# The first layer's two attentions in units of two chunks: a new order of work on five engines

## The chip, the cores and the metric
The kernel runs on one core of a Trainium2 chip. A core has TensorE (PE, matrix products into the banks of PSUM), VectorE (DVE), ScalarE (ACT), GpSimd (POOL) and SyncE (SP, which only issues DMA transfers). Each engine takes its own instructions in order and they wait for each other by semaphores. The metric is the device time of one execution in microseconds, the lower the better.

## The reference
Two transformer layers on x (4 batches, 512 tokens, 256 features) with a context of 1601 rows of 192 features. The change touches the first layer's two attentions:
```python
# layer 0: 16 heads of 64; B = 4, N = 512; S = 512 (self) or 1601 (cross, xc = context)
x = _attn(_ln(x, g1, b1), _ln(x, g1, b1), Wq1, Wk1, Wv1, Wo1, bo1) + x
x = _attn(_ln(x, g2, b2), context, Wq2, Wk2, Wv2, Wo2, bo2) + x
...
    scores = jnp.einsum('bnhd,bshd->bhns', q, k) * scale
    attn = jax.nn.softmax(scores, axis=-1)
    out = jnp.einsum('bhns,bshd->bnhd', attn, v)
```
The second layer has the same with 16 heads of 16. Everything is in float32; the kernel splits q, k and the output into a high and a low part (`q_hi`, `q_lo`, ...) and sums products of the parts.

## The kernel before
The program is a row of phases: projections (`project_phase`), then an attention, five and four in turn. `attend_phase` does self0 (phase a0, 4 chunks of 128 keys) and cross0 (a1, 13 chunks, the last with 65 keys); `attend_narrow` does the second layer's self1 (a2) and cross1 (a3). In a0 and a1 the work is cut into NG = 32 groups of two heads of one batch. For a group:

- Maxima ("items"): for each head, each of the four 128-row pieces of q, and each block of keys (one of 512, or four of 402), TensorE makes scores with all 128 rows, k_hi and k_lo stacked against q_hi twice, into `mx`; VectorE reduces them (L1198).
- `row`: four transposes (L1017) turn a head's maxima into a row of `aux`, and ScalarE copies it, negated, into row 64 of `q_second` (L1131).
- `scores`: per chunk and head two products into a bank of `sc`, the stacked one (L1029) and one of 65 rows, k_hi by q_lo with the maxima subtracted (L1030). ScalarE makes the exp of a bank into `prob` (L1148).
- `values`: per chunk two products, one per head, into the two column halves of `pv` (L1041; each is recorded as two matmuls).
- Sums: GpSimd adds the probabilities of chunk pairs (L977, and L984 in self0), VectorE the last chunk's and the two halves (L1212, L1223 in cross0). Two products with ones (L1056) give the denominators, ScalarE copies them (L1161), VectorE takes reciprocals in four pieces (L1230), multiplies (`divide`, L1246), ScalarE casts the high part (L1168), VectorE subtracts for the low part (L1254), SP stores both.

Each group has U = 2 NCP steps (a chunk pair of one head). In a step TensorE alternates a score with an item of the next group, and the late steps of earlier groups are placed in chosen steps: `value_at`, `DEN_AT`, `RECIP_AT`, `DIVIDE_AT`, `HIGH_AT`, `LOW_AT`. SP loads a group's q, k and v SLOTS - 1 groups ahead (SLOTS 4 or 3), when the values of an earlier one are done. `attend_narrow` already makes maxima for two heads at once in row halves (L1479) and sends them through DRAM (L1380, L1387).

## Time and profile before
| | us |
|---|---|
| median of 3 runs | 3969.08 |
| lowest and highest | 3967.0, 3972.28 |
| the profiled execution | 3972.02 |
| its span, first to last instruction | 3970.2 |
| busy: PE, DVE, ACT, POOL | 3472.6, 2430.1, 2003.7, 1125.2 |
| self0, from the first load to the end (195 to 613): PE busy | 396.48 of 418 |
| cross0 (1025 to 2195): PE busy | 1143.68 of 1170 |

Positions in the trace are microseconds from the span's start. PE is the time in which a matmul was under way; matmuls overlap, so from one's start to the next one's start is what it costs. PEclk is the granted clock of TensorE as a share of 2.4 GHz.

### The profile page before, as it was taken

To read this page: it belongs to the slowest core of one execution; us is meant where nothing else is said; L and a number is where in the kernel's file an instruction comes from. 1 tells how busy PE (TensorE), PEld (TensorE's weight loads), DVE (VectorE), ACT (ScalarE), POOL (GpSimd) and SP (SyncE) were. 2 spreads that over 40 slices of the span, in tenths; PEclk is the share of its full clock that TensorE was granted. 3 is DMA by queue.
4 is the path that set the end of the run, shared out by engine and by line. 5 is a ranking of instruction groups with operands and counts; after the bars stand their busy time and mean duration, and the time that the engine had idled before them with its cause. 6 is when DMAs were issued, how large, how long until landed. Compare 5 with 4: busy or idle time off the path is not lost. (4 is left out here: it accounts for less than half of the span.)

```text
span 3970.2 us, 57943 instructions
## 1 busy us (share of the span) xinstructions
PE 3472.6 (87%) x17596; PEld 2019.0 (51%) x17596; DVE 2430.1 (61%) x4148; ACT 2003.7 (50%) x3541; POOL 1125.2 (28%) x539
## 2 busy tenths in 40 slices
PE   7899995999799999999999588588488599999776
PEld 5644443888455555555554456333366444444254
DVE  4368884443477777777776344386254399999333
ACT  4356662445355555555555223167344168888633
POOL 0056660000366667766667000012000000000000
PEclk8999997999799999999999799789799789999888
DMA  6787766999855555555552432234454522222121
GB/s 213 270 187 194 194 161 247 332 318 312 217 134 134 124 125 132 134 139 122 123 130 57 151 111 96 80 113 133 147 193 139 148 77 87 95 95 100 58 85 42
DMA packets 363425, 590.63 MB, mean 149 GB/s; under 512 B 43675, under 2 KB 196859, under 8 KB 362151
## 3 DMA queue, kind: packets, MB, share of 16 engines
q1 hardware_dynamic: 362312, 586.05, 51.0%
q10 hardware_dynamic: 958, 2.62, 0.4%
q8 instruction: 85, 1.39, 0.1%
q14 instruction: 70, 0.57, 0.0%
HBM read 345.71 MB, written 239.97 MB: 148 GB/s over the span
## 5 line engine op out<-in xcount | busy, mean ns | idle before, releaser
L1198 DVE TENSOR_REDUCE a_blk_max<-a_mx 128x1 f32<-128x402 f32 (+1 forms) x1280 | 734.0, 587 | 430.5 <-PE a_mx L1001 411.5
L1148 ACT ACTIVATE a_prob<-a_sc 128x512 f32<-128x512 f32 (+1 forms) x1088 | 640.1, 597 | 505.1 <-PE a_sc L1030 470.2
L1569 ACT ACTIVATE a_prob<-a_sc 128x512 f32<-128x512 f32 (+1 forms) x1088 | 585.9, 598 | 136.6 <-PE a_sc L1492 131.0
L977 POOL TENSOR_TENSOR a_prob_sum<-a_prob,a_prob_sum 128x1024 f32<-128x1024 f32 x256 | 617.7, 2414 | 62.8 <-ACT a_prob L1148 53.7
L1041 PE MATMUL a_pv<-a_prob,a_v 128*64 128x512 f32 (+1 forms) x2176 | 585.9, 617 | 0.0
L1596 DVE TENSOR_REDUCE a_blk_max<-a_mx 128x1 f32<-128x402 f32 x1024 | 512.1, 568 | 73.6 <-PE a_mx L1479 69.4
L1001 PE MATMUL a_mx<-a_k_stack,a_q_stack 128*128 128x402 f32 (+1 forms) x1280 | 485.0, 389 | 38.2 <-DMA a_q_stack<-q_hi_cross 23.5
L1029 PE MATMUL a_sc<-a_q_stack,a_k_stack 128*128 128x512 f32 (+1 forms) x1088 | 460.5, 423 | 2.1 <-ACT a_q_second L1131 2.1
L1030 PE MATMUL a_sc<-a_q_second,a_k_second 65*128 65x512 f32 (+1 forms) x1088 | 432.1, 397 | 0.0
L977 POOL TENSOR_TENSOR a_prob_sum<-a_prob 128x1024 f32<-128x1024 f32 x128 | 312.1, 2448 | 417.8 <-ACT a_prob L1148 417.8
L1001 PEld LDWEIGHTS a_mx<-a_k_stack,a_q_stack 128*128 128x128 f32 x1280 | 247.8, 194 | 291.7 <-DVE a_blk_max L1198 109.6
L1479 PE MATMUL a_mx<-a_k_stack,a_q_stack 63*128 63x402 f32 (+1 forms) x1280 | 300.5, 409 | 79.9 <-DMA a_q_stack<-a_prob 61.9
L1510 PE MATMUL a_pv<-a_prob,a_v 128*32 128x256 f32 (+2 forms) x4096 | 347.4, 412 | 8.9 <-ACT a_o_full L1548 7.5
L742 DVE TENSOR_TENSOR p_split_lo<-p_ps,p_split_hi 128x512 fp32r<-128x512 f32 (+2 forms) x280 | 171.5, 622 | 296.2 <-ACT p_split_hi L630 295.3
L1029 PEld LDWEIGHTS a_sc<-a_q_stack,a_k_stack 128*128 128x128 f32 (+1 forms) x1088 | 203.2, 187 | 263.5 <-ACT a_prob L1148 132.5
L1492 PE MATMUL a_sc<-a_q_stack,a_k_stack 64*128 64x512 f32 (+1 forms) x1088 | 301.6, 500 | 8.6 <-ACT a_prob L1569 8.5
L630 ACT CAST p_split_hi<-p_ps 128x512 fp32r<-128x512 f32 (+2 forms) x280 | 147.5, 534 | 271.0 <-PE p_ps L355 116.0
L1492 PEld LDWEIGHTS a_sc<-a_q_stack,a_k_stack 64*128 64x128 f32 (+1 forms) x1088 | 118.8, 184 | 254.9 <-ACT a_prob L1569 202.5
L1479 PEld LDWEIGHTS a_mx<-a_k_stack,a_q_stack 63*128 63x128 f32 x1280 | 181.9, 199 | 127.5 <-issue 63.3
L1230 DVE RECIPROCAL a_den<-a_den 128x128 f32<-128x128 f32 x256 | 235.6, 933 | 11.5 <-ACT a_den L1161 11.5
L1455 POOL TENSOR_TENSOR a_o_full<-a_o_full,a_inv 128x512 f32<-128x512 f32 x32 | 40.8, 1276 | 611.6 <-DMA a_inv<-inverse 611.6
L1030 PEld LDWEIGHTS a_sc<-a_q_second,a_k_second 65*128 65x128 f32 (+1 forms) x1088 | 203.0, 187 | 10.6
(248 smaller groups left out, 4911.3 us busy)
## 6 DMA issues: line engine op xcount, KB each, us to landing
a_v<-v_cross SPq DMA_DIRECT2D x48, 768.0 KB
a_k_stack<-k_hi_cross SPq DMA_DIRECT2D x32, 801.0 KB, 6.7
a_k_stack<-k_lo_cross SPq DMA_DIRECT2D x32, 801.0 KB, 9.8
a_k_second<-k_hi_cross SPq DMA_DIRECT2D x32, 801.0 KB
v_cross<-p_v_sb SPq DMA_DIRECT2D x48, 512.0 KB, 4.1
k_hi_cross<-p_split_hi SPq DMA_DIRECT2D x120, 200.0 KB, 3.3
k_lo_cross<-p_split_lo SPq DMA_DIRECT2D x120, 200.0 KB, 3.2
a_q_stack<-q_hi_self SPq DMA_DIRECT2D x64, 256.0 KB, 4.9
```

Source lines behind the costliest of these rows:

```text
L977: nc.gpsimd.tensor_tensor(prob_sum[:, h], prob_of(c, cp, h), other, ALU.add)\
L1001: nc.tensor.matmul(mx[:, (c * NI + m) % MXB, 0:a.blk], qst[r][0:rows, h, t * P:(t + 1) * P], kst[r][0:rows, h, at:at + a.blk], start=True, ...
L1029: nc.tensor.matmul(out, kst[r][:, h, k0:k0 + rows], qst[r][:, h, :], start=True, stop=False)
L1030: nc.tensor.matmul(out, k2[r][0:ROWS, h, k0:k0 + rows], q2[r][0:ROWS, h, :], start=not wide, stop=True).then_inc(st_done, 1)
L1041: last = nc.tensor.matmul(pv[h * M:(h + 1) * M, :], v[r][0:rows, j, h * M:(h + 1) * M], prob_of(c, cp, h)[0:rows, j % 2, :], start=(j == 0 ...
L1148: nc.scalar.activation(prob_of(c, cp, h)[0:rows, k, :], sc[0:rows, (c * E + e) % SCB, :], ACT.Exp, scale=a.scale).then_inc(exp_done, 1)
L1198: nc.vector.reduce_max(blk_max[:, r, h, t, nb:nb + 1], mx[:, (c * NI + n) % MXB, 0:a.blk], AX.X)\
L1479: nc.tensor.matmul(mx[:, g % MXB, 0:a.blk], qst[i % SLOTS][rows, j, t * P:(t + 1) * P], kst[i % SLOTS][rows, j, at:at + a.blk], start=True ...
L1492: nc.tensor.matmul(sc[0:keys, e % SCB, :], kst[i % SLOTS][rows, j, ch * P:ch * P + keys], qst[i % SLOTS][rows, j, :], start=True, stop=Tru ...
L1510: last = nc.tensor.matmul(pv[32 * h:32 * h + 32, cols], v[i % SLOTS][0:keys, ch, 32 * h:32 * h + 32], prob[0:keys, tau % RC, h, cols], sta ...
L1569: nc.scalar.activation(prob[0:keys, tau % RC, m, :], sc[0:keys, e % SCB, :], ACT.Exp, scale=a.scale).then_inc(exp_done, 1)
L1596: nc.vector.reduce_max(dst, mx[:, g % MXB, 0:a.blk], AX.X).then_inc(item_read, 1)
```

## The change
`attend_phase` goes, and `attend_wide` does self0 and cross0. The work is now in units w of two chunks of a group, T = 32 x NCP of them (NCP is 2 in self0 and 7 in cross0).

- TensorE, per unit: four scores (chunk by chunk, head by head), the first part of the unit's maxima, the values of unit w - 1, the denominators if they are due, the rest of the maxima. `pairs_by(w)` says how many pairs of maxima are made by the end of unit w: a group's are complete LEAD = 3 units before it starts. `cut(w)` halves a unit's.
- Maxima: one pair is one piece of q by one block of keys for both heads, the one in rows 0 to 63 and the other in rows 64 to 127, from the high parts alone. The second head's k is stacked the other way round for this.
- VectorE collects the maxima in `row_max`, transposes it in 32 x 32 blocks (`turn`), SP stores it in DRAM and loads it as row 64 of `q_second`; k's row 64 is -1.
- Denominators: two products with ones, into a bank of `mx`. VectorE transposes the bank, takes 16 reciprocals per partition and transposes them back with a broadcast (`invert`). The copy by ScalarE and the long reciprocals go.
- Banks: `mx` 4 and `sc` 3 in both (before 4 and 2 in self0, 3 and 3 in cross0); `aux` goes. SLOTS is 5 in self0 (4 before), 3 in cross0. `sc` is freed by its exp, `prob` (4 or 3 units) by `prob_free`.
- k comes in four transfers of 64 rows instead of two. SP's order per group is in the loop below.
- In `attend_narrow` the scratch for maxima and inverses has another layout, so that rows are read back whole.

The diff, cut to its core:
```diff
-        self.maxima = [dram(f"maxima{n}", [P, 32], F32) for n in range(2)]
-        self.inverse = [dram(f"inverse{n}", [4, NQ], F32) for n in range(2)]
+        self.maxima = [dram(f"maxima{n}", [32, P], F32) for n in range(2)]
+        self.inverse = [dram(f"inverse{n}", [32, P], F32) for n in range(2)]
...
-def attend_phase(pr, name, a):
...
-                sp.dma_start(pr.maxima[n % 2], row_turned[:, n % 2, :]).then_inc(max_stored[n % 2], 16)
+                sp.dma_start(pr.maxima[n % 2].rearrange("c (b i) -> b c i", b=4), row_turned[:, n % 2, :])\
+                    .then_inc(max_stored[n % 2], 16)
...
-                dst = qst[n % SLOTS][63:P:64].rearrange("p j (t b i) -> p (j t) b i", t=4, b=4)
-                src = pr.maxima[n % 2].rearrange("(b x c) i -> x c b i", x=4, c=8)
-                sp.dma_start(words(dst), src[0:2]).then_inc(row_loaded[n % 2], 16)
+                sp.dma_start(words(qst[n % SLOTS][63:P:64]),
+                             pr.maxima[n % 2][0:16].rearrange("(r j t) i -> r j (t i)", r=2, j=2))\
+                    .then_inc(row_loaded[n % 2], 16)
...
-                sp.dma_start(pr.inverse[n % 2].rearrange("h (x i) -> (h x) i", x=32), den[:, n % OS, :])\
+                sp.dma_start(pr.inverse[n % 2][0:16].rearrange("c (y i) -> (c y) i", i=16), den[:, n % OS, :])\
                     .then_inc(inv_stored, 16)
...
-                sp.dma_start(inv[:, n % OS, :], pr.inverse[n % 2].rearrange("(h u) n -> h u n", u=1)
-                             .to_broadcast([4, 32, NQ])).then_inc(inv_loaded[n % OS], 16)
+                rows = pr.inverse[n % 2][0:16].rearrange("(h u c) i -> h u (c i)", h=4, u=1)
+                sp.dma_start(inv[:, n % OS, :], rows.to_broadcast([4, 32, NQ])).then_inc(inv_loaded[n % OS], 16)
...
+def attend_wide(pr, name, a):
...
+    SLOTS = 3 if a.cross else 5
+    RC = 3 if a.cross else 4
+    OS = 3 if a.cross else 4
+    PAIRS = 4 * NB
+    NI = 2 * PAIRS
...
+    MXB, SCB = 4, 3
+    LEAD = 3
+    T = NG * NCP
+    LAST = a.chunk_rows(NC - 1)
+    NV = 1 + (LAST < P)
+    DEN_AT, DIVIDE_AT, HIGH_AT = NCP + 2, NCP + 3, NCP + 4
+    pool_sums = [(cp, h) for cp in range(1, min(NCP, 6)) for h in range(2)]
+    dve_sums = [(cp, h) for cp in range(6, NCP) for h in range(2)]
...
+    def pairs_by(w):
+        return min(NG * PAIRS, -(-PAIRS * (NCP + LEAD + w + 1) // NCP))
+    def cut(w):
+        return (pairs_by(w - 1) + pairs_by(w) + 1) // 2
+    def place(p):
+        return p + sum(cut(i * NCP + DEN_AT) <= p for i in range(NG))
+    def den_place(i):
+        return cut(i * NCP + DEN_AT) + i
...
+        kst = [sb(f"k_stack{s}", [P, 2, KP], F32R) for s in range(SLOTS)]
+        qst = [sb(f"q_stack{s}", [P, 2, NQ], F32R) for s in range(SLOTS)]
+        k2 = [sb(f"k_second{s}", [65, 2, KP], F32R) for s in range(SLOTS)]
+        q2 = [sb(f"q_second{s}", [65, 2, NQ], F32R) for s in range(SLOTS)]
+        v = [sb(f"v{s}", [P, NC, P]) for s in range(SLOTS)]
+        prob = sb("prob", [P, RC, 2, 2, BANK])
+        prob_sum = sb("prob_sum", [P, 2, 2, BANK])
+        CS = 1 if a.cross else 2
...
+        mx = st.enter_context(nc.psum_tensor(f"{name}_mx", [P, MXB, BANK], F32))
+        sc = st.enter_context(nc.psum_tensor(f"{name}_sc", [P, SCB, BANK], F32))
+        pv = st.enter_context(nc.psum_tensor(f"{name}_pv", [P, BANK], F32))
...
+            def load_kq(n):
+                s = n % SLOTS
+                if n >= SLOTS:
+                    sp.wait_ge(st_done, (n - SLOTS + 1) * E)
+                (k_hi, k_lo), q_hi = (t[n] for t in pr.k[a.name]), pr.q[a.name][0][n]
+                for h in range(2):
+                    for half, part in enumerate((k_hi, k_lo) if h == 0 else (k_lo, k_hi)):
+                        sp.dma_start(words(kst[s][64 * half:64 * half + 64, h]), part[64 * h:64 * h + 64])\
+                            .then_inc(loaded[s], 16)
+                for half in range(2):
+                    sp.dma_start(words(qst[s][64 * half:64 * half + 64]), q_hi.rearrange("(h r) s -> r h s", h=2))\
+                        .then_inc(loaded[s], 16)
+            def load_second(n):
+                s, k_hi, q_lo = n % SLOTS, pr.k[a.name][0][n], pr.q[a.name][1][n]
+                for dst, src in ((k2[s], k_hi), (q2[s], q_lo)):
+                    sp.dma_start(words(dst[0:64]), src.rearrange("(h r) s -> r h s", h=2)).then_inc(loaded2[s], 16)
...
+            def store_maxima(n):
+                sp.wait_ge(turned, n + 1)
+                if n >= 2:
+                    sp.wait_ge(row_loaded[n % 2], 16 * (n // 2))
+                sp.dma_start(pr.maxima[n % 2].rearrange("c (b i) -> b c i", b=4), row_turned[:, n % 2, :])\
+                    .then_inc(max_stored[n % 2], 16)
+            def load_maxima(n):
+                sp.wait_ge(max_stored[n % 2], 16 * (n // 2 + 1))
+                sp.dma_start(words(q2[n % SLOTS][64:65]), pr.maxima[n % 2][0:8].rearrange("(o h t) i -> o h (t i)", o=1, h=2))\
+                    .then_inc(row_loaded[n % 2], 16)
...
+            for n in range(SLOTS - 1):
+                load_kq(n)
+                load_second(n)
+                load_v(n)
+                if n == 0:
+                    store_maxima(0)
+                    load_maxima(0)
+            for i in range(NG + 3):
+                if a.cross:
+                    at(load_kq, i + SLOTS - 1)
+                    at(load_second, i + SLOTS - 1)
+                    at(load_v, i + SLOTS - 1)
+                    at(store_maxima, i + 1)
+                    at(load_maxima, i + 1)
+                    at(store, i - 1)
+                else:
+                    at(store_maxima, i + 1)
+                    at(load_maxima, i + 1)
+                    at(load_kq, i + SLOTS - 1)
+                    at(load_second, i + SLOTS - 1)
+                    at(load_v, i + SLOTS - 1)
+                    at(store, i - 3)
...
+            def add(i, m):
+                cp, h = pool_sums[m]
+                pool.wait_ge(exp_done, step_of(i, cp, 1, h) + 1)
+                if cp == 1:
+                    if i:
+                        pool.wait_ge(merged, (i - 1) * 2 + h + 1)
+                    other = prob_of(i * NCP, h)
+                else:
+                    pool.wait_ge(pool_sum, i * len(pool_sums) + m - 1)
+                    other = prob_sum[:, h]
+                nc.gpsimd.tensor_tensor(prob_sum[:, h], prob_of(i * NCP + cp, h), other, ALU.add)\
+                    .then_inc(pool_sum, 1)
+            def merge(i, h):
+                pool.wait_ge(pool_sum, i * 2 + h + 1)
+                if i >= CS:
+                    pool.wait_ge(den_done, i - CS + 1)
+                nc.gpsimd.tensor_tensor(chunk_sum[:, i % CS, h, :], prob_sum[:, h, 0, :], prob_sum[:, h, 1, :], ALU.add)\
+                    .then_inc(merged, 1)
+            for i in range(NG):
+                for m in range(len(pool_sums)):
+                    add(i, m)
+                    if not dve_sums:
+                        merge(i, m)
...
+            def maxima(p0, p1):
+                for p in range(p0, p1):
+                    i, t, nb = pair_of(p)
+                    if p % PAIRS == 0:
+                        pe.wait_ge(loaded[i % SLOTS], 16 * 6 * (i // SLOTS + 1))
+                    for h in range(2):
+                        n = 2 * place(p) + h
+                        if n >= MXB:
+                            pe.wait_ge(item_read, n - MXB + 1)
+                        rows, at = slice(64 * h, 64 * h + 64), a.block_at[nb]
+                        nc.tensor.matmul(mx[:, n % MXB, 0:a.blk], qst[i % SLOTS][rows, h, t * P:(t + 1) * P],
+                                         kst[i % SLOTS][rows, h, at:at + a.blk], start=True, stop=True)\
+                            .then_inc(item_done, 1)
...
+            def scores(w, k, h):
+                i, cp = divmod(w, NCP)
+                s, ch, e = i % SLOTS, 2 * cp + k, step_of(i, cp, k, h)
+                if cp == 0 and k == 0 and h == 0:
+                    pe.wait_ge(loaded2[s], 32 * (i // SLOTS + 1))
+                    pe.wait_ge(row_loaded[i % 2], 16 * (i // 2 + 1))
...
+                if e >= SCB:
+                    pe.wait_ge(exp_done, e - SCB + 1)
+                out = sc[0:keys, e % SCB, :]
+                nc.tensor.matmul(out, kst[s][:, h, k0:k0 + keys], qst[s][:, h, :], start=True, stop=False)
+                nc.tensor.matmul(out, k2[s][:, h, k0:k0 + keys], q2[s][:, h, :], start=False, stop=True)\
+                    .then_inc(st_done, 1)
...
+            def denominators(i):
+                n = 2 * den_place(i)
+                pe.wait_ge(merged, 2 * (i + 1))
+                pe.wait_ge(item_read, n - MXB + 1)
+                for h in range(2):
+                    last = nc.tensor.matmul(mx[64 * h:64 * h + 64, n % MXB, :], pr.ones[:, 0:64],
+                                            chunk_sum[:, i % CS, h, :], start=True, stop=True)
+                last.then_inc(den_done, 1)
...
+            maxima(0, pairs_by(-1))
+            for w in range(T):
+                for ch in a.pair(w % NCP):
+                    for h in range(2):
+                        scores(w, ch % 2, h)
+                maxima(pairs_by(w - 1), cut(w))
+                if w:
+                    values(w - 1)
+                sums_at(w)
+                maxima(cut(w), pairs_by(w))
...
+            def high_part(i):
+                act.wait_ge(divided, i + 1)
...
+            def prob_free(w, h):
+                i, cp = divmod(w, NCP)
+                act.wait_ge(pv_done, i * NC + min(NC, 2 * cp + 2))
+                one = (max(cp, 1), h)
+                if one in pool_sums:
+                    act.wait_ge(pool_sum, i * len(pool_sums) + pool_sums.index(one) + 1)
+                else:
+                    act.wait_ge(dve_sum, i * len(dve_sums) + dve_sums.index(one) + 1)
+            for w in range(T):
+                i, cp = divmod(w, NCP)
+                if cp == 1 and i:
+                    raw_copy(i - 1)
+                if w >= HIGH_AT and (w - HIGH_AT) % NCP == 0:
+                    high_part((w - HIGH_AT) // NCP)
+                for ch in a.pair(cp):
+                    keys = a.chunk_rows(ch)
+                    for h in range(2):
+                        if w >= RC and ch % 2 == 0:
+                            prob_free(w - RC, h)
+                        e = step_of(i, cp, ch % 2, h)
+                        act.wait_ge(st_done, e + 1)
+                        nc.scalar.activation(prob_of(w, h)[0:keys, ch % 2, :], sc[0:keys, e % SCB, :],
+                                             ACT.Exp, scale=a.scale).then_inc(exp_done, 1)
...
+            def turn(i):
+                dve.wait_ge(item_read, 2 * place(i * PAIRS + PAIRS - 1) + 2)
+                if NB > 1:
+                    nc.vector.reduce_max(row_max[:, i % 2, 0:8], blk_max[:, i % 2], AX.X).then_inc(max_done, 1)
...
+                nc.vector.transpose(row_turned[:, i % 2, :], row_max[:, i % 2, :]).then_inc(turned, 1)
...
+            def invert(i):
+                n = 2 * den_place(i)
+                dve.wait_ge(den_done, i + 1)
+                nc.vector.transpose(den[:], mx[:, n % MXB, :]).then_inc(item_read, 2)
+                dve.wait_ge(item_read, n + 2)
+                nc.vector.reciprocal(inv_cols[:], den[:].rearrange("p (k i) -> p k i", i=32)[:, :, 0])\
+                    .then_inc(inverted, 1)
+                dve.wait_ge(inverted, i + 1)
+                nc.vector.transpose(inv[:], inv_cols[:].rearrange("p (k o) -> p k o", o=1).to_broadcast([P, 16, 32]))\
+                    .then_inc(inv_turned, 1)
...
+            def last_sums(i):
+                for n, (cp, h) in enumerate(dve_sums):
+                    rows = a.chunk_rows(2 * cp)
+                    dve.wait_ge(exp_done, step_of(i, cp, 0, h) + 1)
+                    dve.wait_ge(pool_sum, (i + 1) * len(pool_sums) - 2 + h + 1)
+                    nc.vector.tensor_tensor(prob_sum[0:rows, h, 0, :], prob_sum[0:rows, h, 0, :],
+                                            prob_of(i * NCP + cp, h)[0:rows, 0, :], ALU.add).then_inc(dve_sum, 1)
+                if i >= CS:
+                    dve.wait_ge(den_done, i - CS + 1)
+                for h in range(2):
+                    dve.wait_ge(dve_sum, 2 * i + h + 1)
+                    nc.vector.tensor_tensor(chunk_sum[:, i % CS, h, :], prob_sum[:, h, 0, :], prob_sum[:, h, 1, :],
+                                            ALU.add).then_inc(merged, 1)
...
+            def divide(i):
+                dve.wait_ge(pv_copied, i + 1)
+                dve.wait_ge(inv_turned, i + 1)
...
+            blocks(0, pairs_by(-1))
+            for w in range(T + HIGH_AT):
+                blocks(pairs_by(w - 1), cut(w))
+                late(invert, w, DEN_AT)
+                blocks(cut(w), pairs_by(w))
+                if dve_sums:
+                    late(last_sums, w, NCP + 1)
+                late(divide, w, DIVIDE_AT)
+                late(low_part, w, HIGH_AT)
...
         project_phase(pr, "p0", x_in=ins["x"],
                       attn=(SELF0, w0 + "g1", w0 + "b1", w0 + "Wq1", w0 + "Wk1", w0 + "Wv1"))
-        attend_phase(pr, "a0", SELF0)
+        attend_wide(pr, "a0", SELF0)
         project_phase(pr, "p1", x_in=ins["x"], x_out=pr.x, after=(SELF0, w0 + "Wo1", w0 + "bo1"),
                       attn=(CROSS0, w0 + "g2", w0 + "b2", w0 + "Wq2", w0 + "Wk2", w0 + "Wv2"))
-        attend_phase(pr, "a1", CROSS0)
+        attend_wide(pr, "a1", CROSS0)
         project_phase(pr, "p2", x_in=pr.x, x_out=pr.x, after=(CROSS0, w0 + "Wo2", w0 + "bo2"),
                       ff=("geglu", w0 + "g3", w0 + "b3", w0 + "Wp", w0 + "bp", w0 + "Wf", w0 + "bf"),
                       attn=(SELF1, w1 + "n1_g", w1 + "n1_b", w1 + "sq_w", w1 + "sk_w", w1 + "sv_w"))
```

## Rows read from the trace of the kernel before
**Rows 1.** Windows of self0 and cross0 in steady state: busy us (instructions), granted clock, DMA share, GB/s.
```profile
300.00:550.00 250.00, 250.00 (x1071) 122.29 (x1067) 206.59 (x289) 152.65 (x268) 161.56 (x82) 1.00 0.78 193
1200.00:2000.00 800.00, 800.00 (x3350) 409.65 (x3348) 570.97 (x997) 419.08 (x703) 545.03 (x228) 1.00 0.56 131
```
**Rows 2.** Timeline of TensorE in self0: start, us, line, operands, count.
```profile
402.40 1.08 PE L1041 MATMUL a_pv<-a_prob,a_v 128*64 128x512 f32 x4
403.31 1.03 PE L1056 MATMUL a_aux<-a_chunk_sum,ones 128*64 128x512 f32 x4
404.27 0.50 PE L1029 MATMUL a_sc<-a_q_stack,a_k_stack 128*128 128x512 f32 x1
...
404.84 0.39 PE L1001 MATMUL a_mx<-a_k_stack,a_q_stack 128*128 128x512 f32 x1
405.07 0.39 PE L1029 MATMUL a_sc<-a_q_stack,a_k_stack 128*128 128x512 f32 x1
...
405.77 0.60 PE L1017 MATMUL a_aux<-ident,a_blk_max 128*1 128x128 f32 x4
406.30 1.08 PE L1041 MATMUL a_pv<-a_prob,a_v 128*64 128x512 f32 x4
407.31 0.50 PE L1001 MATMUL a_mx<-a_k_stack,a_q_stack 128*128 128x512 f32 x1
...
415.49 1.03 PE L1056 MATMUL a_aux<-a_chunk_sum,ones 128*64 128x512 f32 x4
```
**Rows 3.** Timeline of TensorE in cross0.
```profile
1488.16 1.03 PE L1056 MATMUL a_aux<-a_chunk_sum,ones 128*64 128x512 f32 x4
...
1514.52 0.34 PE L1001 MATMUL a_mx<-a_k_stack,a_q_stack 128*128 128x402 f32 x1
1514.70 0.40 PE L1029 MATMUL a_sc<-a_q_stack,a_k_stack 128*128 128x512 f32 x1
...
1523.48 1.03 PE L1056 MATMUL a_aux<-a_chunk_sum,ones 128*64 128x512 f32 x4
```
**Rows 4.** Groups by line in cross0, 1200 to 2000: busy us, mean ns, idle before.
```profile
L1198 DVE TENSOR_REDUCE a_blk_max<-a_mx 128x1 f32<-128x402 f32 x725 | 404.9, 567 | 227.6 <-PE a_mx L1001 214.0
...
L1212 DVE TENSOR_TENSOR a_prob_sum<-a_prob_sum,a_prob 65x512 f32<-65x512 f32 x44 | 28.1, 679 | 0.0
L1246 DVE TENSOR_TENSOR a_o_full<-a_o_full,a_den 128x512 f32<-128x512 f32 x23 | 22.3, 971 | 0.0
```
**Rows 5.** Groups by line in self0, 300 to 550.
```profile
L1148 ACT ACTIVATE a_prob<-a_sc 128x512 f32<-128x512 f32 x166 | 94.4, 595 | 24.8 <-PE a_sc L1030 17.9
...
L1246 DVE TENSOR_TENSOR a_o_full<-a_o_full,a_den 128x512 f32<-128x512 f32 x20 | 27.4, 1369 | 0.0
```
**Rows 6.** Timeline at the start of self0 and of cross0.
```profile
194.60 0.74 SPq L926 DMA_DIRECT2D a_k_stack<-k_hi_self  x1
...
201.93 3.99 PE L1001 MATMUL a_mx<-a_k_stack,a_q_stack 128*128 128x512 f32 x8 [12.75 <-DMA a_q_stack<-q_hi_self]
...
207.13 0.47 PE L1029 MATMUL a_sc<-a_q_stack,a_k_stack 128*128 128x512 f32 x1 [0.77 <-ACT a_q_second L1131]
...
1037.76 15.81 PE L1001 MATMUL a_mx<-a_k_stack,a_q_stack 128*128 128x402 f32 x32 [23.46 <-DMA a_q_stack<-q_hi_cross]
...
1055.19 0.76 PE L1029 MATMUL a_sc<-a_q_stack,a_k_stack 128*128 128x512 f32 x1 [0.77 <-ACT a_q_second L1131]
```
**Rows 7.** Timeline of TensorE in cross1, two pairs and the product after them.
```profile
3401.68 0.70 PE L1479 MATMUL a_mx<-a_k_stack,a_q_stack 63*128 63x402 f32 x4
3402.31 0.64 PE L1510 MATMUL a_pv<-a_prob,a_v 128*32 128x256 f32 x8
```
**Rows 8.** Timeline of TensorE in self1, after an idle piece.
```profile
2659.24 0.50 PE L1479 MATMUL a_mx<-a_k_stack,a_q_stack 63*128 63x512 f32 x2 [1.79 <-DMA a_q_stack<-q_lo_self]
```
**Rows 9.** Window of self1 just after it: busy us, granted clock, DMA share, GB/s.
```profile
2659.80:2663.20 3.40, 3.40 (x22) 1.13 (x20) 2.57 (x5) 1.59 (x3) 0.06 (x1) 0.50 0.03 11
```
**Rows 10.** DMA issues in cross1, 3200 to 3700: count, KB, median us to landing.
```profile
maxima<-a_row_turned SPq DMA_DIRECT2D x14, 16.0 KB, 1.4
```

556 lines of the change are left out of this document (122 added, 434 removed).

## The prediction
> **What bounds the kernel now.** I read the windows first, at the two attentions of the first layer, which the change rewrites. [rows 1] In steady state TensorE is busy 250.00 of 250.00 us in the self attention and 800.00 of 800.00 us in the cross attention, at a granted clock of 1.00. VectorE is busy 83% and 71%, ScalarE 61% and 52%, GpSimd 65% and 68%. TensorE is the bound, and only what is on TensorE, or stops it, sets the time. The period of a group (two heads of one batch; 32 groups) I take from two neighbouring denominator products: 415.49 - 403.31 = 12.18 us in the self attention [rows 2], 1523.48 - 1488.16 = 35.32 us in the cross attention [rows 3]. The DMA engines are 78% busy in the self attention [rows 1], so a faster TensorE would soon meet them.
>
> **TensorE's work per group.** [rows 2] An item of 512 columns takes 405.07 - 404.84 = 0.23 us; from 405.07 to 405.77 there are a score (two matmuls) and an item, 0.70, so a score is 0.47. The four transposes that turn a head's maxima take 0.53 (405.77 to 406.30). Values of a chunk take 1.01 (406.30 to 407.31), but 0.91 where the denominators follow in the same 128*64 tiles (402.40 to 403.31). The first score after such a product takes 0.57 (404.27 to 404.84), not 0.47. So leaving the column tiles costs 0.10 + 0.10, and I take 0.10 for entering (an estimate, from the same rows); a visit is 0.3. In 402 columns an item takes 0.18 [rows 3].
>
> Self attention: eight items become four pairs of two products in the two row halves. In the second layer's kernel, which does so already, four such matmuls (two pairs) take 0.63 to the next product [rows 7], 0.31 a pair with the way into column tiles in it, so 0.19 to 0.27; I take one item's time for a pair, which removes 4 x 0.23 = 0.93. The row turns go, 2 x 0.53; each was also the way into column tiles, which now costs 0.1 elsewhere, so 0.87. Values of two chunks stand together: 2 visits instead of 4 save 0.6. But a pair lies in 64-row tiles between full-array scores and column tiles: 4 changes more at 0.1, +0.4. The denominators are the same two products. 12.18 - 0.93 - 0.87 - 0.6 + 0.4 = 10.2 us. Cross attention: 16 x 0.18 = 2.9, 0.87, and 6 visits fewer, 1.8, go; 14 changes at 0.1 come, and 0.2 for units with two pairs side by side: 35.32 - 2.9 - 0.9 - 1.8 + 1.4 + 0.2 = 31.3 us.
>
> No row shows a 64-row product between a full-array one and a column one. If that change were free, the sums would be 9.8 and 29.9; if each cost 0.2, 10.6 and 32.7. The row that speaks to it is 405.77 to 406.30: full-array transposes that follow full-array items pay nothing, though the data type changes, so it is the tiles that cost [rows 2]. The Trainium skill, "TensorEngine Tiling (Array Packing)", Key Properties, says that a change of tiling mode drains TensorE; by that rule all four changes of a unit are paid, as I have them, and without it the sums would be the lower pair.
>
> **What stops TensorE: the order of turns.** The old code alternates a score with an item and has its late steps between them. The new one works in units of two chunks: four scores, maxima, values of the unit before, (denominators), maxima. ScalarE is in order, and with three banks (`SCB = 3`) the fourth score waits for the unit's first exp. Unhindered, that score begins 3 x 0.47 = 1.4 us into the unit and the exp is over just then.
> (a) `high_part(i)` stands ahead of the exps of unit HIGH_AT. It waits for `divide(i)`, which stands on VectorE at the end of unit HIGH_AT - 1, behind that unit's last pair, and TensorE issues this pair last, directly before the next unit's scores. From the start of those scores, self attention: the pair ends at 0.15, two reductions of 0.6 (estimate from 0.57 at 402 columns [rows 4]) to 1.35, divide 1.37 [rows 5] to 2.7, the cast like a 0.60 exp [rows 5] to 3.35, first exp to 3.95. TensorE stands 3.95 - 1.4 = 2.55 us in each group. Cross attention: reductions to 1.25, `turn` falls into the same unit (estimate 0.4, a reduction of 32 numbers and a 32-column transpose, of which the 0.57 of [rows 4] is an upper bound each), divide 0.97 [rows 4], cast and exp: 3.85, so 2.45. Behind the wait lie all four exps, hence the last score, the maxima and the values.
> (b) Cross attention alone: probabilities have three buffers; the exps of unit cp = 2 wait for VectorE's `last_sums` over the buffer of the last chunk. They stand at the end of unit cp = 1: 1.25 + 0.68 [rows 4] + exp 0.6 = 2.55, less 1.4: 1.15. GpSimd's next additions wait for the merges behind it, but ten of 2.4 us (24.1 of 35.3 us busy [rows 1]) still fit.
> (c) VectorE waits for the denominators with reductions behind: 0.2 in the cross attention, an estimate; I cost the two new transposes beside TensorE. No row has one of 512 columns: at the 0.57 of a reduction or the 1.37 of the slowest divide they replace four reciprocals, and with 1.37 they lengthen (a) by up to 0.5. Taken: the reduction's.
> Periods: 10.2 + 2.55 = 12.75 us and 31.3 + 2.45 + 1.15 + 0.2 = 35.1 us.
>
> **The clock.** In the second layer's self attention an idle piece of 1.79 us (2657.45 to 2659.24 [rows 8]) was followed by 3.4 us at a granted clock of 0.50, the 1.2 GHz level [rows 9]; all the while TensorE had work, so 1.7 us of it was lost. In (a) it stands 2.3 us after the third score's tail. Unknown is how often: never 0, always 1.7. I take every third group, 0.55, below the middle of the two, as these attentions have no other idle around the stop. So 13.3 and 35.7 us.
>
> **The DMA loop.** Maxima now go through DRAM. `load_maxima` blocks SP until the store has landed, and the store is queued behind the loads and stores already issued; loads of the next group are issued only after it. In the self attention a group's transfers fill 0.78 x 12.18 = 9.5 us [rows 1], a small store on an empty queue lands after 1.4 [rows 10], and the next load's first bytes take up to another 1.4: 12.3 us. That is under 12.75, so it sets nothing unless TensorE stops less. k now comes in four 64-partition pieces; bytes are the same, and I leave the time of a load alone (bounds: 2 us less if halves overlap, 1 more for four more issues). The Trainium skill, "SBUF — State Buffer", Door 1, gives 64 partitions only half the ports and about 218 GB/s; by that the 1.6 MB of k and q alone take 7.2 us, and the 193 GB/s of the whole window agree. In the cross attention the loads (0.56 busy) are hidden by 35 us of products.
>
> **The starts.** Before, scores begin when one group's maxima are done: 207.13 and 1055.19 [rows 6]. Now 10 pairs (2.5 groups) and 23 pairs (1.4 groups) come first, and SP issues group 1 only after maxima 0 have been stored. Self attention: 201.93 + 8 reductions 4.9 + turn 0.4 + store, wait and load 2.1 = 209.3; k and q of a group take 201.93 - 194.60 = 7.3, so 216.6; the rest of group 1 and k and q of group 2, 1.84 MB at 193 to 220 GB/s, to 226: +19 us. Cross attention: 1037.76 + 15.8 + 0.4 + 1.5 = 1055.5; twice the bytes, 14 us; seven more pairs 5.5: 1075, +20 us.
>
> **The sum.** Self: +19, 29 periods x (13.3 - 12.18) = +32, last three groups without maxima and so without (a) about -7: +44. Cross: +20, 30 x (35.7 - 35.32) = +11, the end -6: +25. In the second layer only the loads of the maxima get simpler, 64 small packets to four rows: -2, bounds -5 and 0. Together +67 us. The profiled execution took 3972.02 us, 3 above the median of 3969.08, so 4039 on its scale and 4036 us predicted.
>
> **Rivals.** A measurement of this kernel can tell about 0.2%, 8 us.
> 1. Forecast: stops and some clock falls, 4036, own range 4000 to 4080. Chance 0.48.
> 2. The same stops, clock never down: 0.55 less in 59 periods, -33: 4003. The idle pieces are long enough to speak against it. 0.15.
> 3. Clock down in nearly every group: +1.15 each, +68: 4104. For it: (a) repeats in all groups, and is longer than 1.79. 0.15.
> 4. The other side: the last pair's reductions and the divide are through early, ScalarE never holds the fourth score, and TensorE stays filled. Self is then held by the DMA loop at 12.4 (+19 + 6 - 7 = +18), cross runs at 31.5 (+20 - 115 - 6 = -101): 3884. It decides once the cross period is under 33.4 us, that is, the stops (a) to (c) cost under 2.1 instead of 3.8. Against it: the order on three engines is fixed by the code. 0.10.
> 5. As 4, and the DMA loop hides too, self at 10.4: 29 x -1.8 + 12 = -40: 3826. 0.05.
> What lies between, within 0.2%: 0.07.
> Faster: 4 and 5, 0.15, and 0.02 of case 2, should its stops be shorter; same 0.07; slower 0.76. The range leaves out case 5, half of 4 and the end of 3: 3895 to 4125.
>
> **What would show it.** After: periods between denominator products of 13.3 and 35.7 us; TensorE idle about 2.3 us before the fourth score of one unit per group, ended by an exp, which had waited for the cast, that for the divide; in the cross attention a second, 1.2 us, ended through L1212's successor; clock under 1.00 in both windows; first scores 19 and 20 us later; VectorE's reciprocals gone. Wrong if TensorE is still over 97% busy in those windows, if the idle pieces end by DMA (then the loop is the bound), or if a unit's products alone take more than 10.6 and 32.7 us a group.

## The result, and the profile after

After: 4284.3 us median (4281.0 to 4292.0, 4 runs). Before, beside it: 3970.7 us (3967.0 to 3976.6). The ratio is 1.0793, with a 95% interval of 1.0779 to 1.0807: 314 us slower, where I forecast 67. The direction was right, the size was not. Some executions of a kernel take over 1.5% longer than its fastest one; ratios and intervals leave these out, medians below are of all its runs.

The steady windows of the changed kernel, in the columns of [rows 1]:

```profile
300.00:550.00 250.00, 193.33 (x654) 79.78 (x654) 157.62 (x205) 79.01 (x149) 112.25 (x58) 0.80 0.54 141
1300.00:2100.00 800.00, 708.90 (x2773) 310.22 (x2772) 480.73 (x854) 295.56 (x556) 477.10 (x198) 0.92 0.48 115
```

TensorE was busy all the time at a clock of 1.00 [rows 1]. Now it stands 23% of the self attention and 11% of the cross attention, and the mean clock is down as well, to 0.80 and 0.92 (third figure from the end). No other engine and no transfer comes near to full: something waits in a chain. The last denominator products of each attention, before and then after, say where the time went:

```profile
602.48 1.97 PE L1056 MATMUL a_aux<-a_chunk_sum,ones 128*64 128x512 f32 x4 [2.98 <-POOL a_chunk_sum L984]
...
2184.00 1.08 PE L1056 MATMUL a_aux<-a_chunk_sum,ones 128*64 128x512 f32 x4 [2.52 <-DVE a_chunk_sum L1223]
```

```profile
749.01 1.98 PE L1319 MATMUL a_mx<-a_chunk_sum,ones 128*64 128x512 f32 x4 [4.02 <-POOL a_chunk_sum L1273]
...
2500.53 1.97 PE L1319 MATMUL a_mx<-a_chunk_sum,ones 128*64 128x512 f32 x4 [4.25 <-DVE a_chunk_sum L1443]
```

The self attention lost 749.01 - 602.48 = 146.5 us (forecast 44), the cross attention, from 2500.53 - 2184.00 = 316.5, another 316.5 - 146.5 = 170.0 (forecast 25), and the rest of the program gained 3 (forecast 2). One group of the self attention, TensorE's timeline; these rows answer to [rows 2]:

```profile
402.41 0.80 PE L1310 MATMUL a_sc<-a_q_stack,a_k_stack 128*128 128x512 f32 x1 [4.04 <-ACT a_prob L1391]
...
407.48 1.02 PE L1319 MATMUL a_mx<-a_chunk_sum,ones 128*64 128x512 f32 x4
408.44 0.50 PE L1294 MATMUL a_mx<-a_k_stack,a_q_stack 64*128 64x512 f32 x2
408.87 0.50 PE L1310 MATMUL a_sc<-a_q_stack,a_k_stack 128*128 128x512 f32 x1
...
410.38 0.51 PE L1310 MATMUL a_sc<-a_q_stack,a_k_stack 128*128 128x512 f32 x1
...
411.05 0.49 PE L1294 MATMUL a_mx<-a_k_stack,a_q_stack 64*128 64x512 f32 x2
411.47 1.94 PE L1333 MATMUL a_pv<-a_prob,a_v 128*64 128x512 f32 x8
413.34 0.50 PE L1294 MATMUL a_mx<-a_k_stack,a_q_stack 64*128 64x512 f32 x2
413.77 0.50 PE L1310 MATMUL a_sc<-a_q_stack,a_k_stack 128*128 128x512 f32 x1
...
419.48 0.80 PE L1310 MATMUL a_sc<-a_q_stack,a_k_stack 128*128 128x512 f32 x1 [4.04 <-ACT a_prob L1391]
...
424.55 1.02 PE L1319 MATMUL a_mx<-a_chunk_sum,ones 128*64 128x512 f32 x4
```

The period is 424.55 - 407.48 = 17.07 us, and from 339 to 715 us it is that 22 times running. An undisturbed unit reaches its fourth score after 410.38 - 408.87 = 1.51 us. The unit with the cast needs 419.48 - 413.77 = 5.71, so the stop costs 4.20. VectorE, ScalarE and GpSimd beside it:

```profile
410.31 1.25 DVE L1415 TENSOR_REDUCE a_row_max<-a_mx 128x1 f32<-128x512 f32 x2
...
411.73 2.56 DVE L1454 TENSOR_TENSOR a_o_lo<-a_o_full,a_o_hi 128x512 fp32r<-128x512 f32 x1
414.21 2.47 DVE L1415 TENSOR_REDUCE a_row_max<-a_mx 128x1 f32<-128x512 f32 x4
416.60 1.67 DVE L1449 TENSOR_TENSOR a_o_full<-a_o_full,a_inv 128x512 f32<-128x512 f32 x1
...
418.31 0.62 ACT L1367 CAST a_o_hi<-a_o_full 128x512 fp32r<-128x512 f32 x1 [6.52 <-DVE a_o_full L1449]
418.83 1.56 ACT L1391 ACTIVATE a_prob<-a_sc 128x512 f32<-128x512 f32 x3
...
411.38 2.36 POOL L1266 TENSOR_TENSOR a_prob_sum<-a_prob 128x1024 f32<-128x1024 f32 x1 [9.05 <-ACT a_prob L1391]
...
415.39 2.34 POOL L1266 TENSOR_TENSOR a_prob_sum<-a_prob 128x1024 f32<-128x1024 f32 x1
```

The chain is the one forecast: exponentials behind the cast, cast behind the divide. Its links are longer. The low part of 128x512 takes 2.56 us, and its end lies 0.55 behind the end of GpSimd's addition (411.38 + 2.36 = 413.74; 411.73 + 2.56 = 414.29). The divide ends 0.54 behind the next one (417.73; 418.27). So each seems to run only when an addition of GpSimd is over. The cross attention, the same stop:

```profile
1801.66 14.41 POOL L1266 TENSOR_TENSOR a_prob_sum<-a_prob,a_prob_sum 128x1024 f32<-128x1024 f32 x6
...
1805.01 0.50 PE L1310 MATMUL a_sc<-a_q_stack,a_k_stack 128*128 128x512 f32 x1
...
1806.56 2.65 DVE L1449 TENSOR_TENSOR a_o_full<-a_o_full,a_inv 128x512 f32<-128x512 f32 x1
...
1810.42 0.79 PE L1310 MATMUL a_sc<-a_q_stack,a_k_stack 128*128 128x512 f32 x1 [3.73 <-ACT a_prob L1391]
```

The fourth score comes 5.41 us into its unit, 3.9 late. Groups take 39.3 to 41.1 us, 40.4 in the mean. The windows around the self attention's stop, and then the one at the cross attention's stop, clock third from the end:

```profile
410.35:417.44 7.09, 5.08 (x21) 2.21 (x20) 7.05 (x10) 1.44 (x3) 5.98 (x3) 1.00 0.23 82
417.44:424.27 6.83, 4.79 (x12) 1.79 (x14) 2.12 (x3) 2.68 (x5) 1.88 (x2) 0.50 0.64 166
424.27:434.50 10.23, 8.23 (x34) 3.60 (x30) 8.70 (x12) 2.65 (x5) 5.98 (x3) 1.00 0.47 122
...
1810.08:1816.91 6.83, 6.49 (x17) 2.19 (x17) 2.05 (x5) 1.86 (x4) 5.99 (x3) 0.50 0.01 2
```

In each of those 22 groups of the self attention, 2.0 us after TensorE went idle (at 415.4), the clock goes to 0.50, the 1.2 GHz level, for 6.83 us, twice the 3.4 of [rows 9]. The first 2.0 us of that lie in the stop, and TensorE works for 4.79. In the cross attention the clock falls in every group too, for 6.83 us in 25 of the first 30 and for 3.41 in the other five, which are the groups of 39.3 us. In the fall shown TensorE works for 6.49 us.

### The profile page after: what moved, and what is told of

Its sections match the earlier page's. It is cut to its first block and busy times, and to the rows that moved or that the text cites. A ratio compares the mean times of both kernels' runs of the same rounds, so it can differ in the third digit from the quotient of the medians.

```text
span 4283.6 us, 50963 instructions
## 1 busy us (share of the span) xinstructions
PE 3505.2 (82%) x17084; PEld 1919.0 (45%) x17084; DVE 2408.5 (56%) x4116; ACT 1821.4 (43%) x3349; POOL 1126.7 (26%) x542
## 5 line engine op out<-in xcount | busy, mean ns | idle before, releaser
L1391 ACT ACTIVATE a_prob<-a_sc 128x512 f32<-128x512 f32 (+1 forms) x1088 | 576.6, 599 | 737.0 <-PE a_sc L1311 616.7
L1415 DVE TENSOR_REDUCE a_blk_max<-a_mx 128x1 f32<-128x402 f32 x1024 | 530.8, 568 | 476.4 <-PE a_mx L1294 472.8
L1310 PE MATMUL a_sc<-a_q_stack,a_k_stack 128*128 128x512 f32 (+1 forms) x1088 | 506.3, 465 | 248.2 <-ACT a_prob L1391 248.1
L1046 ACT ACTIVATE a_prob<-a_sc 128x512 f32<-128x512 f32 (+1 forms) x1088 | 585.7, 598 | 137.9 <-PE a_sc L969 132.9
L1333 PE MATMUL a_pv<-a_prob,a_v 128*64 128x512 f32 (+1 forms) x2176 | 619.3, 695 | 0.0
L1073 DVE TENSOR_REDUCE a_blk_max<-a_mx 128x1 f32<-128x402 f32 x1024 | 512.2, 567 | 73.3 <-PE a_mx L956 68.8
L1311 PE MATMUL a_sc<-a_q_second,a_k_second 65*128 65x512 f32 (+1 forms) x1088 | 449.1, 413 | 0.0
L1294 PE MATMUL a_mx<-a_k_stack,a_q_stack 64*128 64x402 f32 (+1 forms) x1280 | 318.8, 500 | 69.1 <-DMA a_q_stack<-q_hi_cross 39.4
L1294 PEld LDWEIGHTS a_mx<-a_k_stack,a_q_stack 64*128 64x128 f32 x1280 | 136.1, 209 | 441.8 <-issue 204.0
L1333 PEld LDWEIGHTS a_pv<-a_prob,a_v 128*64 128x64 f32 (+1 forms) x2176 | 147.2, 153 | 263.7 <-issue 160.6
L1415 DVE TENSOR_REDUCE a_row_max<-a_mx 128x1 f32<-128x512 f32 x256 | 160.3, 676 | 125.2 <-PE a_mx L1294 125.2
L1311 PEld LDWEIGHTS a_sc<-a_q_second,a_k_second 65*128 65x128 f32 (+1 forms) x1088 | 215.1, 198 | 26.7
```

The source lines that it names most:

```text
L1046: nc.scalar.activation(prob[0:keys, tau % RC, m, :], sc[0:keys, e % SCB, :], ACT.Exp, scale=a.scale).then_inc(exp_done, 1)
L1073: nc.vector.reduce_max(dst, mx[:, g % MXB, 0:a.blk], AX.X).then_inc(item_read, 1)
L1294: nc.tensor.matmul(mx[:, n % MXB, 0:a.blk], qst[i % SLOTS][rows, h, t * P:(t + 1) * P], kst[i % SLOTS][rows, h, at:at + a.blk], start=True ...
L1310: nc.tensor.matmul(out, kst[s][:, h, k0:k0 + keys], qst[s][:, h, :], start=True, stop=False)
L1311: nc.tensor.matmul(out, k2[s][:, h, k0:k0 + keys], q2[s][:, h, :], start=False, stop=True)\
L1333: last = nc.tensor.matmul(pv[64 * h:64 * h + 64, :], v[i % SLOTS][0:keys, ch, 64 * h:64 * h + 64], prob_of(w, h)[0:keys, ch % 2, :], start ...
```

## The experiments

Theory A is the forecast's: the order of turns makes the stop. Its supplement, called A1 or D in the expectations: VectorE's instructions with two inputs from SBUF wait until GpSimd pauses. Rivals: B, the products became longer; C, the loop of transfers. Each kernel has runs of the kernel before beside it (medians of 3960.6 to 3970.8 us). Where no interval is given, there is one timed run. Where some groups are long and others not, one run says little within tens of us: experiment 1 gave 4043.7 to 4116.0 us in five. All edits are to `attend_wide` of the changed kernel.

**1. The cast behind the exponentials.**

```diff
             for w in range(T):
...
-                if w >= HIGH_AT and (w - HIGH_AT) % NCP == 0:
-                    high_part((w - HIGH_AT) // NCP)
                 for ch in a.pair(cp):
...                      # the four exponentials
+                if w >= HIGH_AT and (w - HIGH_AT) % NCP == 0:
+                    high_part((w - HIGH_AT) // NCP)
```

> ScalarE casts the high half of a group after the four exponentials of the unit instead of ahead of them; nothing else moves. Theory A (the order of the turns makes the stop: exponentials behind cast, cast behind divide, divide behind the last reductions): the idle time of TensorE ahead of the fourth score (4.0 us of a group in the first attention, 3.7 in the second) goes, and with it most of the half-clock stretches (6.83 us a group). First attention 17.07 us a group down to 10.7 by the products alone, or to about 12.4 if the loop of transfers then ends last; second 40.7 - 3.9 - 3.2 = 33.6. In all 4284 - 31 x 4.7 - 31 x 7.1 = about 3920 us. Theory B (the new tile shapes and the dense denominators make the products themselves longer): the stop may go, but the groups stay above 15 and 38 us, over 4170 in all. Theory C (the loop of loads on the queue sets the first attention): first attention unchanged near 17, the second as in theory A, about 4065.

Measured 4059.6 us (4043.7 to 4116.0, 5 runs), ratio to before 1.0201 (1.018 to 1.022): 140 us above the 3920 of theory A. Even so, one move gave back 225 of the 314 us. The stop on the exponentials is gone. The self attention fell to 11.9 us a group in the mean, as by theory A with C behind it. In the cross attention most groups took 34.5, but eight of 31 took 44 to 46, which none of the theories had. One of those, GpSimd and VectorE:

```profile
1721.35 13.94 POOL L1266 TENSOR_TENSOR a_prob_sum<-a_prob,a_prob_sum 128x1024 f32<-128x1024 f32 x6
...
1726.23 9.61 DVE L1449 TENSOR_TENSOR a_o_full<-a_o_full,a_inv 128x512 f32<-128x512 f32 x1
1735.76 1.53 DVE L1415 TENSOR_REDUCE a_blk_max<-a_mx 128x1 f32<-128x402 f32 x3
```

The divide stands through four additions until GpSimd's row is over (1735.29) and ends 0.55 behind it, 1735.84. TensorE then waited 7.02 us for a reduction, and the clock was down for 13.65 us.

**2. The stop filled with other work.** In the unit with the cast, before the fourth score:

```diff
+                        if ch % 2 and h and w >= HIGH_AT and (w - HIGH_AT) % NCP == 0:
+                            repeat_product(pairs_by(w - 1), 14)   # next maxima product, same bank
                         scores(w, ch % 2, h)
```

> In the unit with the cast, TensorE repeats the next maxima product 14 times ahead of the fourth score, into the bank that this product writes anyway, so that most of the stop is filled with work; the chain cast behind divide stays. The question is what the clock costs apart from the wait. If the half clock comes from the stop: granted clock back to about 1.0 in both attentions, the wait itself stays, and a group falls by what the clock took, 2.2 us in the first attention (17.07 to about 14.9) and 3.2 in the second (40.7 to about 37.5), 4284 - 68 - 99 = about 4117 us. If the clock falls for another reason: granted clock stays at 0.80 and 0.92 and the time stays near 4284 or above it, by up to 1 us a group where the repeats overrun the stop.

Measured 4317.3 us, 200 above the 4117 expected and 33 above the changed kernel. In the self attention the mean clock rose from 0.80 to 0.92 and a group fell from 17.07 to between 14.9 and 16.6. The groups of 14.9 are those without a fall of the clock; the others had one of 3.41 us, though no idle piece of TensorE was over 0.7. In the cross attention it missed: 42.2 to 43.2 us, clock 0.92, as the divide now took 4.7 to 5.0 us in 28 of 30 groups (in one of them beside two additions). Inconclusive there, so it was repeated in another way (experiment 12).

**3. GpSimd's additions made small.** They cover 16 columns; most of the denominators' sum is left out.

```diff
-                nc.gpsimd.tensor_tensor(prob_sum[:, h], prob_of(i * NCP + cp, h), other, ALU.add)
+                nc.gpsimd.tensor_tensor(prob_sum[:, h, :, 0:16], prob_of(i * NCP + cp, h)[:, :, 0:16],
+                                        other, ALU.add)
...                      # `other` and the merge are cut to 16 columns in the same way
```

> GpSimd's additions cover 16 of the 512 columns (the rest of the sums holds a constant, so most of the denominators' sum is left out); counts, order and waits stay. Theory A1 (VectorE's divide and low part wait out a whole GpSimd addition beside them): the divide goes from 1.7 to 2.7 us to about 0.7, the low part from 2.6 to about 0.7, the stop from 4.0 to about 2 in the first attention and from 3.7 to about 1.8 in the second; a group 2 and 2 us shorter at least, 4284 - 62 - 62 = about 4160, and down to about 4030 if the half-clock stretches go too. If GpSimd has no part in it: divide and low part as before, time within 10 us of 4284.

Measured 4097.5 us. VectorE's divide and low part in the self attention, 350 to 550, and then in the cross attention, 1500 to 2000, by line (busy us, mean ns of one):

```profile
L1452 DVE TENSOR_TENSOR a_o_full<-a_o_full,a_inv 128x512 f32<-128x512 f32 x14 | 9.5, 681 | 0.0
L1457 DVE TENSOR_TENSOR a_o_lo<-a_o_full,a_o_hi 128x512 fp32r<-128x512 f32 x14 | 9.1, 650 | 0.0
...
L1457 DVE TENSOR_TENSOR a_o_lo<-a_o_full,a_o_hi 128x512 fp32r<-128x512 f32 x14 | 9.5, 681 | 0.0
L1452 DVE TENSOR_TENSOR a_o_full<-a_o_full,a_inv 128x512 f32<-128x512 f32 x13 | 8.4, 650 | 0.0
```

With GpSimd nearly idle they take 0.65 to 0.68 us, in place of 1.67 and 2.56 in the self attention, 2.65 and 0.68 in the cross attention. TensorE's waits shrank to 1.5 and 1.8 us. With the order unchanged, GpSimd's neighbourhood is worth 187 us, clock included; what is left, 127 us over the kernel before, does not hang on it. The Trainium skill, "SBUF — State Buffer", SBUF: two separate sides, says that VectorE with two SBUF inputs and GpSimd exclude each other: whichever starts first holds the port for its whole instruction, and the other is blocked. The trace agrees for one instruction: the low part above ended 0.55 us behind the addition that it met. The 9.61 us go beyond it, as VectorE did not get in after any of the first three of four additions.

**4. The divide ahead of its unit's first reductions**, the cast left where the change has it.

```diff
             for w in range(T + HIGH_AT):
+                late(divide, w, DIVIDE_AT)
                 blocks(pairs_by(w - 1), cut(w))
                 late(invert, w, DEN_AT)
                 blocks(cut(w), pairs_by(w))
...
-                late(divide, w, DIVIDE_AT)
```

> VectorE divides a group ahead of the first reductions of its unit instead of behind the last ones; the cast stays ahead of the exponentials. Theory A: the divide comes some four reductions (2.5 us) earlier in the first attention and six or more in the second, so the cast is no longer late in the second (stop of 3.7 us gone, clock back, 40.7 to about 33.6 us a group) and late by 1.7 us at most in the first (17.07 to 12.4 to 14.6). In all 4284 - 31 x 3.6 - 31 x 7.1 = about 3950 us. Theory B or C as for the cast moved late: over 4170, or the first attention unchanged and about 4065.

Measured 4024.5 us. Cross 33.8 to 33.9 us in all steady groups but two (35.8 and 34.1), at clock 1.00 (33.6 expected), divide 1.94 us; self 14.1 to 15.0, at the upper end of what was expected and past it, with 1.74 us of stop left and the clock at 0.85. So the total missed the expected 3950 by 75. Experiments 1 and 4 undo the chain at its two ends. The first takes stop (a) away in both attentions, the second in the cross attention, and in the self attention it leaves 1.74 of 4.04 us. Theory A holds. B falls as the cause of the stop; that the products are longer as well, by less, is counted below.

**5. Both orders at once.**

> Both orders at once: divide ahead of the first reductions of its unit, cast behind the exponentials. In the run with the divide first alone the second attention took 33.87 us a group in every group and the first 14.5; with the cast late alone 11.4 to 15.7 in the first, and 34.5 with every fifth group at 45.5 in the second, where one divide stood 9.61 us beside four GpSimd additions in a row. Theory D (VectorE's instructions with two inputs from SBUF wait until GpSimd pauses, so their place among its additions decides): the divide keeps the place of the run where it took 1.94 us, no group at 45.5, second attention 33.9 throughout; first as with the cast late, 11.9 in the mean. 4069 - 31 x 3.05 = about 3974 us. Rival: the long divides come with the late cast itself, groups of 45 us stay and the time is near 4070.

Measured 3969.3 us, 3974 expected. Cross 33.9, no long divide. Self 13.6 us in 16 groups in a row, 1.7 more than expected, and 11.9 to 12.3, about as expected, in most of those before and after. One group of either kind and one from behind the row:

```profile
289.04:300.99 11.95, 11.26 (x47) 4.90 (x45) 10.84 (x15) 5.22 (x10) 8.01 (x5) 1.00 0.63 175
396.84:410.47 13.63, 12.89 (x46) 5.29 (x44) 10.84 (x14) 5.21 (x10) 8.01 (x4) 0.88 0.67 177
571.04:582.99 11.95, 11.22 (x46) 4.89 (x44) 10.85 (x15) 5.21 (x10) 8.01 (x5) 1.00 0.81 199
```

VectorE, ScalarE and GpSimd (third to fifth busy time) work for the same time in all three, and TensorE stands for 0.7 us in each. What differs is the clock: it is down for 3.41 us in each group of the row, and half of that is the 1.7 us. So the total matched by luck: the self attention's mean of 12.34 is 0.44 us above the 11.9 expected, about 14 us in all, and the cross attention gained 3.5 us a group instead of 3.05, about 15. Whether the early divide hurts or helps the self attention once the loop of transfers is mended (experiment 6), no run shows; the later kernels leave it late there.

**6. A load moved on the queue**, on top of 1, self attention only.

```diff
                     at(store_maxima, i + 1)
-                    at(load_maxima, i + 1)
                     at(load_kq, i + SLOTS - 1)
+                    at(load_maxima, i + 1)
```

> The cast behind the exponentials, and in the first attention the queue of loads takes the key and query loads of a later group between the store of the row maxima and their load, which waits for that store. With the cast late alone this load waited 4.5 us in each of 21 groups (5.5 at most). If the loop of transfers holds the first attention there: groups of 14 and 15 us go, the mean falls from 11.86 to about 11.0, the wait to under 1 us, 4069 - 27 = about 4040 us. If VectorE's low part (2.56 us beside an addition) and the late reductions behind it hold it: the mean stays within 0.3 of 11.86 and the time within 10 us of 4069.

Measured 3984.4 us, 56 better than expected. Not all of that is the edit's: the cross attention, which it doesn't touch, had four long groups in the profiled execution where that of experiment 1 had eight, and was 52 us shorter. The self attention ended 38.5 us earlier. The queue's own waits in 350 to 550 (us in total, times, longest), first as in experiment 1 and then here:

```profile
SPq L1210 <- DMA maxima<-a_row_turned: 76.4, 16, 5.5
```

```profile
SPq L1210 <- DMA maxima<-a_row_turned: 4.7, 2, 3.1
```

The self attention fell to 10.5 us a group in the mean (10.6 to 11.4, 10.9 in the mean, in steady state; the last groups, without maxima, are shorter), TensorE busy 199.68 of 200 us at clock 1.00. So behind the stop the loop of transfers was the next bound (rival C, second in line). The load of the maxima had waited 76.4 / 16 = 4.8 us each time for their 16 KB store, and the queue stood with it; in the second layer, with fewer loads about, such a store lands after 1.4 us [rows 10]. That it is the loads ahead of it which make it late is likely, but no run separates that.

**7. Sums early on top of 4**, cross attention: VectorE's `last_sums` ahead of the second half of the reductions.

```diff
                 late(invert, w, DEN_AT)
+                if dve_sums:
+                    late(last_sums, w, NCP + 1)
                 blocks(cut(w), pairs_by(w))
-                if dve_sums:
-                    late(last_sums, w, NCP + 1)
```

> The divide ahead of the first reductions (cast where the change has it), and in the second attention VectorE adds the last chunk and the two halves ahead of the second half of the unit's reductions, one turn earlier. The stop that is left there is 0.82 us a group, ended by an exponential that waits 3.7 us for VectorE's last addition. Expected: 33.87 to about 33.05 us a group, 4023 - 26 = about 3997 us, first attention unchanged at 14.5. Rival: the additions come early enough but push the reductions back, so that the maxima products stand 0.8 us instead; no change in time.

Measured 4026.7 us. Groups of 32.87 us, one less as expected, but six of 31 at 39.9 to 40.6 beside them, each with a low part of 9.0 us: no gain in sum, in a way that neither expectation had.

**8. Experiments 1 and 3 together** (most of the denominators' sum left out).

> The cast behind the exponentials, with GpSimd's additions over 16 of 512 columns (most of the denominators' sum left out). Theory D: no divide above 1 us and no low part above 1 us, the groups of 45.5 us in the second attention gone, all at about 34.5 (36.92 in the mean before), the first attention at 10.7 to 11.4, or at what the loop of transfers gives; 4069 - 75 - 25 = about 3970 us. Rival: the long groups come from the waits on the exponentials or from transfers, and stay with GpSimd nearly idle: about 4060.

Measured 3948.1 us. No divide or low part above 0.7 us, and the cross groups at 33.8 but for one of 35.7: the groups of 45 us were GpSimd's. The self attention, still with the old queue order, had groups up to 16.0, so the long ones there were not GpSimd's.

**9 to 11. Adding up.** Experiment 9 is 1 and 6, with 4 in the cross attention alone; 10 adds the early sums; 11 adds to 9 a new start:

```diff
-            for n in range(SLOTS - 1):
-                load_kq(n)
-                load_second(n)
-                load_v(n)
-                if n == 0:
-                    store_maxima(0)
-                    load_maxima(0)
+            first = min(SLOTS - 1, 3)
+            for n in range(first):
+                load_kq(n)
+            load_second(0)
+            store_maxima(0)
+            load_maxima(0)
+            load_v(0)
...                      # then the rest, group by group
```

> The best order of each attention: cast behind the exponentials in both; in the first the queue loads keys and queries between the store and the load of the maxima; in the second the divide stands ahead of its unit's first reductions. Theory D and the transfer loop add up: first attention 10.5 us a group as with the load between, second 33.4 as with the divide first, 3984 - 31 x 1.85 = about 3927 us, below the kernel before (3961 to 3966). If they do not add up (the gain of one makes the other's wait): 3955 or more.

> The kernel of both orders, with VectorE's last additions ahead of the second half of the unit's reductions in the second attention. Without the late cast this took the 0.82 us stop of every group away (33.87 to 32.87 us), but one group in eight grew to 40.4 us, so the sum was zero. If those groups came from a long divide or low part that held ScalarE's exponentials through the cast, they stay away now: 3927 - 31 x 1.0 = about 3896 us. If VectorE's additions themselves wait for a row of GpSimd's additions: they come again, and the time is within 10 us of the kernel of both orders.

> The kernel of both orders; at the start of each attention the queue issues the keys and queries of the first groups (three in the first attention, two in the second) ahead of the store of the first maxima, on whose turn it otherwise stands (8 us in the first attention). The change's 2.5 and 1.4 groups of maxima ahead of the first score then wait for no load behind that store. First attention's first score from 226.8 us to about 215, the second's likewise about 12 earlier: 3927 - 24 = about 3903 us. If the first scores are late for the products and reductions themselves and not for the loads: under 5 us each, 3917 or more.

Measured 3920.3, 3897.6 and 3901.4 us against 3927, 3896 and 3903 expected. The gains add up. The first score of the self attention came at 215.5 instead of 227.5 us, so the changed start was held by loads issued behind the store of the first maxima. The early sums still left two of 31 groups near 40.6 us.

**Full rows instead of halves**, on top of 9: each product of a pair covers all 128 rows.

```diff
-                        rows, at = slice(64 * h, 64 * h + 64), a.block_at[nb]
+                        rows, at = slice(0, P), a.block_at[nb]
```

> The kernel of both orders, with each maxima product over all 128 rows (the high and the low half of the keys) instead of two products side by side in two row halves. A pair in halves now takes 0.43 us to the next product and makes the first score behind it 0.34 instead of 0.235; two full products are 2 x 0.233 = 0.47 with no change of tiles beside a score, and the visit of column tiles then costs 0.1 to 0.2 instead. If the change of tiles eats what the row halves give: time within 12 us of the kernel of both orders, about 3927. If the halves do give what I predicted (0.93 us a group in the first attention and 2.9 in the second, less 0.4 and 1.4 for changes): 31 x 0.5 + 31 x 1.5 = 62 us slower, about 3990.

Measured 3931.4 us, 11 more than experiment 9, within the 12 expected if the change of tiles eats the gain; self 10.48 us a group in the mean against 10.47, cross 34.1 against 33.85. The two row halves, a main part of the change, are worth nothing in the one attention and 0.25 us in the other.

**12. The stop filled without touching VectorE**: the third score is repeated in place.

```diff
+                again = 7 if k == 1 and h == 0 and w >= HIGH_AT and (w - HIGH_AT) % NCP == 0 else 0
+                for _ in range(again):
+                    nc.tensor.matmul(out, kst[s][:, h, k0:k0 + keys], qst[s][:, h, :], start=True, stop=False)
+                    nc.tensor.matmul(out, k2[s][:, h, k0:k0 + keys], q2[s][:, h, :], start=False, stop=True)
```

> The changed kernel as it is, but in the unit with the cast the third score is computed eight times in place (seven repeats of 0.47 us, 3.3 us) before its exponential may read it, so that TensorE works through most of the stop and no bank or wait of VectorE is touched. In the second attention the earlier fill met a divide of 5.03 us and the clock still fell in every group, so what the clock costs there is still open. If the half clock comes from the stop: granted clock near 1.0 in both, 17.07 to about 14.9 us and 40.7 to about 37.5 us a group, 4284 - 67 - 99 = about 4118 us; the divide keeps its 1.7 and 2.65 us. If the clock falls for the other, shorter stops too: it stays at 0.80 and 0.92 and the time near 4284.

Measured 4254.8 us. Windows 350 to 550 and 1500 to 2000:

```profile
350.00:550.00 200.00, 188.45 (x779) 100.00 (x778) 146.38 (x188) 69.23 (x133) 108.95 (x56) 1.00 0.60 159
1500.00:2000.00 500.00, 467.13 (x1909) 220.62 (x1908) 321.63 (x535) 183.19 (x346) 296.53 (x124) 0.97 0.48 116
```

In the self attention the clock is at 1.00 and the group at 14.90 us, as forecast, with the fourth score as late as before (5.76 us into its unit). So of 17.07 the clock took 2.17, and filling the stop with products over the full array kept it up: repeats that compute nothing new made the group faster. Standing is not all that counts, though: in experiment 2, whose repeats have 64 rows, TensorE stood 0.7 us at a time as well (0.82 here), and the clock still fell in two groups of three. In the cross attention seven of 29 groups took 37.5 to 38.1 (37.5 expected), without a fall of the clock; in these the divide took 2.4 to 2.7 us, as in the changed kernel. The others took 41.6 to 43.2, with a divide of 5.0. So the total missed by 137 us. The same instruction, with nothing changed on its own engine, took twice as long.

**13. All that helped**: 9, early sums and the new start.

> All that helped, together: cast behind the exponentials, the queue's order in the first attention, divide first and sums early in the second, loads ahead of the first maxima's store at the starts. If the gains are independent: 3920 less 23 (sums early) less 19 (starts) = about 3879 us, 2.2 per cent under the kernel before (3966). If the earlier start only moves the wait (the starts and the sums share a cause): 3895 or more.

Measured 3896.0 us, ratio 0.981 (0.979 to 0.984), 17 above the 3879 expected, with runs from 3883 to 3946. In the profiled one five of 31 cross groups took 40.1 to 40.7. Two neighbouring groups of the cross attention, the low part and GpSimd's row around it:

```profile
1522.51 17.28 POOL L1271 TENSOR_TENSOR a_prob_sum<-a_prob,a_prob_sum 128x1024 f32<-128x1024 f32 x7
1530.83 2.08 DVE L1459 TENSOR_TENSOR a_o_lo<-a_o_full,a_o_hi 128x512 fp32r<-128x512 f32 x1
...
1555.36 16.79 POOL L1271 TENSOR_TENSOR a_prob_sum<-a_prob,a_prob_sum 128x1024 f32<-128x1024 f32 x7
1563.70 9.00 DVE L1459 TENSOR_TENSOR a_o_lo<-a_o_full,a_o_hi 128x512 fp32r<-128x512 f32 x1
```

The same instruction at the same place (8.32 and 8.34 us into the row) got in behind one addition and then only behind the whole row, which was four.

**14. GpSimd pauses once a group**, on top of 13.

```diff
                 cp, h = pool_sums[m]
+                if a.cross and i and (cp, h) == (4, 0):
+                    pool.wait_ge(o_lo_done, i)
```

> As the kernel with all that helped, but in the second attention GpSimd's seventh of ten additions of a group waits until VectorE's low part of the group before is done. With all that helped, most groups of the second attention took 32.9 us and about one in six 40.1 to 40.7; in one of these the low part stood 9.00 us beside four additions (2.08 in the group before, beside the same row). If the row of additions without a gap is the cause: no low part over 2.5 us, no group over 34 us, mean 33.68 to about 32.9, 3896 - 24 = about 3872 us, and the runs lie closer together than 3883 to 3946. If the long low parts have another cause: they stay, 3896 or, with GpSimd now later, above it.

Measured 3875.6 us (3867.9 to 3878.3, 5 runs), ratio to before 0.9751 (0.973 to 0.977), 3872 expected. The divide and the low part by line, and the window, 1500 to 2000:

```profile
L1456 DVE TENSOR_TENSOR a_o_full<-a_o_full,a_inv 128x512 f32<-128x512 f32 x15 | 10.5, 702 | 0.0
L1461 DVE TENSOR_TENSOR a_o_lo<-a_o_full,a_o_hi 128x512 fp32r<-128x512 f32 x15 | 10.2, 681 | 0.0
```

```profile
1500.00:2000.00 500.00, 499.89 (x2130) 225.78 (x2129) 336.89 (x656) 221.50 (x426) 362.73 (x151) 1.00 0.59 142
```

All steady groups take 32.8 to 33.1 us, TensorE is busy 499.89 of 500. The intervals of experiments 13 and 14 do not overlap. A wait added to an engine that was 70% busy made the kernel faster, and 2.5% faster than before the change.

## Why the forecast had the direction and not the size

By its own steps, self attention first:

| term | forecast, self / cross | measured | from |
|---|---|---|---|
| work on TensorE | 10.2 / 31.3 us | 10.7 to 10.9 / 32.9 | 14.90 - 4.20 (experiment 12), steady groups of 6; experiment 14 |
| stop (a) | 2.55 / 2.45 | 4.20 / 3.9 | rows of the changed kernel |
| stop (b) | - / 1.15 | - / 1.0 | experiments 4 and 7 (33.87 - 32.87) |
| clock | 0.55 / 0.55 | 2.17 / about 2.6 | experiment 12: 17.07 - 14.90, 40.4 - 37.8 |
| period | 13.3 / 35.7 | 17.07 / 40.4 | rows of the changed kernel |
| start | +19 / +20 | +19.7 / +20.3 | first scores against [rows 6] |

- **Work** was 0.5 and 1.6 us short: I took the middle of what a change of tiles costs. In the self attention's group above, a pair takes 0.42 to 0.43 us to the next product, where I took one item's 0.23, and the score behind it is longer too (0.34 for 0.23). My own row said so: 0.31 us a pair [rows 7], but of 402 columns, which makes 0.39 of 512. The upper bound of the forecast (10.6 and 32.7) is a little passed, and that was one of its signs of being wrong. The kernel with full rows agrees: what the halves gain, the changes of tiles take back.
- **Stop (a)** is the step that failed, in its durations. Self: the reductions ended 2.91 us into the unit (416.68 - 413.77) instead of 1.35, as the low part of the group before, which I had left out of VectorE's queue, stood 2.56 us ahead of them; the divide ended at 4.50, not at 2.7. Cross: the divide began at 1.55, within 0.1 of the forecast, and took 2.65 instead of 0.97. I had both durations from the kernel before, where they fell among other neighbours. Alone they are 0.65 to 0.68; they are not properties of the instruction but of its place beside GpSimd.
- **The clock** was the other failed step. I gave it to every third group at 1.7 us; rival 3, nearly every group, had 0.15 and was right about how often, but the fall lasted 6.83 us, not 3.4, and cost 2.2 and 2.6. In the self attention 4.79 of the 6.83 us were work and the rest lay in the stop, so half of 4.79, 2.4, is the most it could cost.
- **The sum** of these: 17.07 - 13.3 = 3.8 and 40.4 - 35.7 = 4.7 us a group; with 26 and 29 steady periods 98 and 136 us, of the 247 by which the forecast was short. The other 13 us lie in the first and last groups and are not split further.
- **Not shown**: I read the 193 GB/s of the self attention's window as in agreement with 218 GB/s for pieces of 64 partitions. The transfers were busy 0.78 of that window [rows 1], so 193 is a mean with pauses in it and settles nothing.
- **Right**: the chain and its order (exp, cast, divide, last reductions), the second stop in the cross attention, both starts, that the loop of transfers stands directly behind the stop, and that rival 4's condition (stops gone) gives a kernel below 3969. Rival 4 was priced 3884 with the self attention at 12.4 and its products at the forecast's length; experiment 9, which is that case with the queue mended too, gave 3920, experiment 14 3876. That the last is near 3884 is luck: the products are longer than in the rival's sum, and the mended queue and start are not in it.
- **Open**: what lets a waiting VectorE instruction in between two additions in one group and not in the next, and what makes the clock fall in one group and not in another with the same work and the same idle time.

## What to carry to other kernels

An in-order engine that has a long chain's last link ahead of the work that feeds TensorE makes the whole chain a stop; put such late steps behind the urgent ones, and look through every queue that the chain crosses, small transfers behind large ones too. The duration of a VectorE instruction with two SBUF inputs, read from a trace, holds for that place alone: find out what GpSimd does beside it, and if GpSimd works in rows without a pause, give it one wait where VectorE comes by. A stop that recurs in every group costs its length and then the clock's share again, here half to two thirds of it on top (2.17 on 4.20, 2.6 on 3.9).

## What the runs showed of the hardware

- One VectorE instruction of 0.65 us stood 9.61 us, over the rest of a row of GpSimd additions, and ended 0.55 us after the row (experiment 1). In the changed kernel it ended as long behind a single addition: the divide 0.54 in both attentions (in the cross attention 1809.21, the addition 1808.67).
- The clock fell in every steady group with a stop of 4.04 or 3.73 us, 2.0 us (self, in most groups) or 2.1 to 3.9 us (cross) after TensorE went idle: for 6.83 us in the self attention, for 6.83 or 3.41 in the cross attention. It also fell in every steady self group of experiment 4, where the stop was 1.73 us.
- Stops of 0.82 us came in every steady cross group of experiments 4, 5 and 9 and in every steady self group of experiment 12, and the clock stayed at 1.00. A stop of 1.09 us in the seventh cross group was met by a fall of 3.41 us in experiments 4 and 5 (35.8 us) and by none in experiment 9 (34.1 us).
- But in experiment 5 the clock fell in 16 self groups in a row (3.41 us at 0.50 of 13.65), where the longest idle piece of TensorE was 0.6 us, and stayed at 1.00 in the groups before and after, with the same pieces. The row began behind a group with a piece of 2.09 us. In experiment 2 it fell in about two self groups of three, with pieces of 0.7 us. The length of an idle piece alone does not decide; what does, no run here shows.
- Work that TensorE computes for nothing can be cheaper than standing: experiment 12 runs 14 extra matmuls in each self group and is 2.17 us a group faster there.
